# An expert feed-forward stage: first product turned with its weight streamed from DRAM, second product in three rounded passes

## What is computed

```python
xn = (x - mu) * rsqrt(var + EPS) * gamma + beta
probs = softmax(einsum('btd,ed->bte', xn, router_w) / TEMP)
w, idx = top_k(probs, 2)
wdense = sum(one_hot(idx, E) * w[..., None], axis=-2)
h = silu(einsum('btd,edf->betf', xn, W1))
y = einsum('betf,efd->betd', h, W2)
out = einsum('bte,betd->btd', wdense, y) + res
```

## Time and profile before

| | us |
|---|---|
| median of 3 runs | 3400.73 |
| lowest and highest run | 3398.74, 3401.56 |
| span of the profiled execution (first to last instruction) | 3399.2 |
| time of the profiled execution | within the 3 runs above; its profile gives the span alone |
| PE busy in the span | 3002.1 (88%) |
| PE weight loads, DVE, ACT, POOL busy | 1930.5, 1799.6, 1368.2, 1139.2 |
| mean granted clock of TensorE | 0.942 of full |

### The profile page before, as it was taken

One profiled execution on the slowest core, in us unless ns is written; L12 is line 12 of the kernel. 1 busy time (PEld: TensorE's weight loads), 2 busy tenths in 40 slices (PEclk: granted clock), 3 DMA queues, 4 the chain that ended last, 5 costly groups with the idle time before them and its releaser, 6 DMA issues. The chain is left out here.

```text
span 3399.2 us, 47089 instructions
## 1 busy us (share of the span) xinstructions
PE 3002.1 (88%) x17554; PEld 1930.5 (57%) x17554; DVE 1799.6 (53%) x2965; ACT 1368.2 (40%) x2304; POOL 1139.2 (34%) x995
## 2 busy tenths in 40 slices
PE   7779999999999979999988795999687878899877
PEld 6645555555555438888874564766465565344345
DVE  6656565565655654224229654111256758666565
ACT  3334444444444434324323462333232635355554
POOL 0126565665666650000006331333133413121232
PEclk9889999999999989999999896999898899799989
DMA  1100000000000001111100107221200100000000
GB/s 56 53 1 1 1 1 1 1 1 1 1 1 1 1 15 57 50 32 56 50 23 0 35 1 254 34 35 32 53 2 7 28 7 10 2 1 1 1 29 29
DMA packets 108641, 81.89 MB, mean 24 GB/s; under 512 B 22283, under 2 KB 102181, under 8 KB 108421
## 3 DMA queue, kind: packets, MB, share of 16 engines
q1 hardware_dynamic: 94693, 65.15, 6.3%
q0 software_dynamic: 7488, 9.48, 1.7%
q10 hardware_dynamic: 6240, 4.26, 0.4%
HBM read 68.31 MB, written 11.47 MB: 23 GB/s over the span
## 5 line engine op out<-in xcount | busy, mean ns | idle before, releaser
L787 POOL TENSOR_TENSOR acc<-acc,pf 128x512 f32<-128x512 f32 (+1 forms) x448 | 564.0, 1281 | 255.2 <-ACT pf L914 255.2
L971 DVE TENSOR_REDUCE mxa<-ps 128x1 f32<-128x512 f32 x512 | 327.0, 680 | 229.9 <-PE ps L833 227.9
L914 ACT ACTIVATE pf<-ps 128x512 f32<-128x512 f32 x512 | 277.9, 595 | 318.8 <-PE ps L808 293.4
L821 PE MATMUL ps<-pf,v 128*64 128x512 f32 (+1 forms) x1152 | 311.6, 619 | 0.0
L3635 ACT ACTIVATE pT<-ps 128x1024 f32<-128x1024 f32 (+1 forms) x192 | 154.1, 811 | 130.4 <-PE ps L3553 129.8
L3647 DVE TENSOR_REDUCE mx<-ps 128x2 f32<-128x1024 f32 (+1 forms) x192 | 174.8, 950 | 42.4 <-PE ps L3540 36.7
L1168 POOL TENSOR_TENSOR x<-x,ys 128x256 f32<-128x256 f32 x16 | 11.8, 738 | 509.0 <-DVE ys L1373 509.0
L833 PE MATMUL ps<-kH,qH 64*128 64x512 f32 x512 | 158.1, 442 | 23.7 <-DVE mc L979 18.5
L1786 POOL TENSOR_TENSOR e<-e,sm 128x1232 f32<-128x1232 f32 x48 | 107.9, 2247 | 174.6 <-DVE sm L2050 174.6
L2495 DVE TENSOR_SCALAR ys<-ps,xs 128x256 f32<-128x256 f32 x39 | 18.9, 484 | 251.4 <-PE ps L2314 251.4
L811 PE MATMUL ps<-qH,kH 64*128 64x512 f32 (+1 forms) x576 | 144.3, 475 | 1.5 <-ACT pf L914 0.8
(11 more groups left out here) (554 smaller groups left out, 6959.6 us busy)
## 6 DMA issues: line engine op xcount, KB each, us to landing
w_raw<-in_c_h SPq DMA_DIRECT2D x32, 512.0 KB, 4.0
w1a<-in_f_w SPq DMA_DIRECT2D x8, 1024.0 KB, 13.8
w2a<-in_f_w SPq DMA_DIRECT2D x8, 1024.0 KB, 12.8
w_raw<-in_c_w SPq DMA_DIRECT2D x32, 128.0 KB, 2.2
x<-in_x SPq DMA_DIRECT2D x1, 2048.0 KB, 8.4
moe_rows<-rowbuf ACTq DMA_DIRECT2D x4, 512.0 KB, 10.4
moe_acc<-x ACTq DMA_DIRECT2D x1, 2048.0 KB, 13.1
x<-moe_acc SPq DMA_DIRECT2D x1, 2048.0 KB, 8.2
```

What stands on the lines that cost most here:

```text
L787: pool.tensor_tensor(now[0:r, :], now[0:r, :], pf[0:r, n % RING, a, :], ALU.add).then_inc(added.sem, 1)
L821: ins = pe.matmul(g.bk(3)[SIDE[a], :], v[0:r, u // 2 % 2, t, u % 2 * P + a * HD:u % 2 * P + (a + 1) * HD], pf[0:r, n % RING, a, :], start= ...
L914: act.activation(pf[0:r, n % RING, a, :], g.bk(bk.bank[f"s{n}_{a}"])[0:r, :], ACT.Exp, bias=bias)\
L971: dve.tensor_reduce(mxa[:, q % 2, half, a, j:j + 1], g.bk(4 + a), AXX, ALU.max).then_inc(bk.release(f"m{q}_{i}_{a}"), 1)
```

## The change

- `hidden` is turned. W1 is now stationary (128x128 blocks, 16 of them) and the rows `xT` are the moving operand with 128 columns. The product comes out with the hidden dimension on the partitions, so that `turn_hidden` and its PSUM fills are gone. The four PSUM banks 0 to 3 alternate between tiles.
- W1 is no longer held in SBUF. After `indexed`, SP loads the 1 MB W1 of the tile's expert for every tile into a ring of three (`w1r`, events `w1_in`); tile i's load waits for the end of `hidden(i - 3)`. All eight W2 are still loaded at the start.
- `output` takes three passes over rounded parts: with hi the fp32r rounding of a value and lo the fp32r rounding of the rest, it adds h_hi W2_hi, h_hi W2_lo and h_lo W2_hi, 24 matmuls of 256 columns in fp32r.
- ACT makes W2_hi (a copy of the expert's 2048 columns to fp32r) and applies SiLU twice to each half, once to fp32r and once to float32. DVE makes W2_lo and the two halves of h_lo by subtraction.
- PE's order in iteration i is `turn_rows(i + 1)`, `hidden(i)`, `output(i - 1)`. ACT does `rows_out(i + 1)` first, then W2_hi, then the SiLUs. DVE does the three subtractions of tile i before `weighted(i - 1)`.

```diff
@@ -2157,7 +2157,12 @@
-        w1a, w2a = sb("w1a", [P, E8 * KD, H]), sb("w2a", [P, E8 * HB, D])
+        W1_RING = 3
+        w1r, w2a = sb("w1r", [P, W1_RING, KD, H]), sb("w2a", [P, E8 * HB, D])
+        w2s = [sb(f"w2_{n}", [P, 2, HB, D], F32R) for n in ("hi", "lo")]
+        hs = [sb(f"hT_{n}", [P, 2, HB, P], F32R) for n in ("hi", "lo")]
+        PASSES = ((0, 0), (0, 1), (1, 0))
+        f32 = lambda t: t.bitcast(F32)
...
-        h, hT = sb("h", [P, 2, H]), sb("hT", [P, 2, HB, P])
+        h, hT = sb("h", [P, 2 * H]), zT[:].rearrange("p a k n -> p (a k n)").rearrange("p (a f n) -> p a f n", a=2, n=P)
...
         for i in range(N + 1):
-            if i < N:
-                fills += [(f"a{i}_0", 0), (f"a{i}_1", 1)]
             if i + 1 < N:
                 fills += [(f"x{i + 1}", 6 + (i + 1) % 2)]
+            if i < N:
+                fills += [(f"a{i}_0", 2 * (i % 2)), (f"a{i}_1", 2 * (i % 2) + 1)]
             if i:
                 fills += [(f"y{i - 1}", 4 + (i - 1) % 2)]
-            if i < N:
-                fills += [(f"h{i}_0", 2), (f"h{i}_1", 3)]
...
-        first_in, w_in, stored = g.ev("w_loaded", 16 * 3), g.ev("expert_loaded", 32 * E8), g.ev("x_stored", 16)
+        first_in, w_in, stored = g.ev("w_loaded", 16 * 3), g.ev("expert_loaded", 16 * E8), g.ev("x_stored", 16)
...
+        w1_in = [g.ev(f"raw_loaded{r}", 16 * len(range(r, N, W1_RING))) for r in range(W1_RING)]
+        w2_hi, w2_lo, h_lo = g.ev("w_hi_made", N), g.ev("w_lo_made", N), g.ev("g_lo_made", 2 * N)
...
@@ -2221,8 +2226,13 @@
                 for e in range(E8):
-                    load(sp, w1a[:, e * KD:(e + 1) * KD, :], rows(W1[e]), w_in)
                     load(sp, w2a[:, e * HB:(e + 1) * HB, :], rows(W2[e]), w_in)
+                sp.wait_ge(*indexed.at(0, 1))
+                for i in range(N):
+                    e = sp.value_load(texp[0:1, i:i + 1], min_val=0, max_val=E8 - 1)
+                    if i >= W1_RING:
+                        sp.wait_ge(*bk.full(f"a{i - W1_RING}_1", 0))
+                    sp.dma_start(w1r[:, i % W1_RING], W1[ds(e, 1)].rearrange("a (k p) n -> p (a k) n", p=P)).then_inc(w1_in[i % W1_RING].sem, 16)
...
@@ -2287,32 +2297,28 @@
-                def hidden(i, e):
+                def hidden(i):
                     pe.wait_ge(*bk.read(f"x{i}", 0))
+                    pe.wait_ge(*w1_in[i % W1_RING].at(0, 16 * (i // W1_RING + 1)))
                     for half in range(2):
+                        out = g.bk(2 * (i % 2) + half)
                         pe.wait_ge(*bk.free(f"a{i}_{half}", 0))
-                        for k in range(KD):
-                            ins = pe.matmul(g.bk(half), xT[:, i % 2, k, :],
-                                            w1a[:, ds(e * KD + k, 1), half * CH:(half + 1) * CH].rearrange("p a n -> p (a n)"),
-                                            start=k == 0, stop=k == KD - 1)
-                        ins.then_inc(bk.fill(f"a{i}_{half}"), 1)
-
-                def turn_hidden(i):
-                    for half in range(2):
-                        pe.wait_ge(*bk.read(f"a{i}_{half}", 0))
-                        pe.wait_ge(*bk.free(f"h{i}_{half}", 0))
                         for f in range(HB // 2):
                             at = half * CH + f * P
-                            ins = pe.transpose(g.bk(2 + half)[:, f * P:(f + 1) * P], h[:, i % 2, at:at + P], g.ident[:])
-                        ins.then_inc(bk.fill(f"h{i}_{half}"), 1)
-
-                def output(i, e):
+                            for k in range(KD):
+                                ins = pe.matmul(out[:, f * P:(f + 1) * P], w1r[:, i % W1_RING, k, at:at + P], xT[:, i % 2, k, :],
+                                                start=k == 0, stop=k == KD - 1)
+                        ins.then_inc(bk.fill(f"a{i}_{half}"), 1)
+
+                def output(i):
                     pe.wait_ge(*bk.free(f"y{i}", 0))
+                    pe.wait_ge(*w2_lo.at(0, i + 1))
                     for f in range(HB):
                         if f % (HB // 2) == 0:
-                            pe.wait_ge(*bk.read(f"h{i}_{f // (HB // 2)}", 0))
-                        ins = pe.matmul(g.bk(4 + i % 2)[:, 0:D], hT[:, i % 2, f, :],
-                                        w2a[:, ds(e * HB + f, 1), :].rearrange("p a n -> p (a n)"), start=f == 0, stop=f == HB - 1)
+                            pe.wait_ge(*h_lo.at(0, 2 * i + f // (HB // 2) + 1))
+                        for p, (sh, sw) in enumerate(PASSES):
+                            ins = pe.matmul(g.bk(4 + i % 2)[:, 0:D], hs[sh][:, i % 2, f, :], w2s[sw][:, i % 2, f, :],
+                                            start=f == 0 and p == 0, stop=f == HB - 1 and p == len(PASSES) - 1)
@@ -2340,19 +2346,13 @@
-                pe.wait_ge(*w_in.at(0, 32 * E8))
-                last = None
                 for i in range(N + 1):
-                    if i < N:
-                        e = pe.value_load(texp[0:1, i:i + 1], min_val=0, max_val=E8 - 1)
-                        hidden(i, e)
                     if i + 1 < N:
                         turn_rows(i + 1)
+                    if i < N:
+                        hidden(i)
                     if i:
-                        output(i - 1, last)
-                    if i < N:
-                        turn_hidden(i)
-                        last = e
@@ -2387,18 +2387,22 @@
+                act.wait_ge(*w_in.at(0, 16 * E8))
+                act.wait_ge(*indexed.at(0, 1))
                 for i in range(N):
+                    if i + 1 < N:
+                        rows_out(i + 1)
+                    e = act.value_load(texp[0:1, i:i + 1], min_val=0, max_val=E8 - 1)
+                    if i >= 2:
+                        act.wait_ge(*bk.full(f"y{i - 2}", 0))
+                    act.activation(w2s[0][:, i % 2], w2a[:, ds(e * HB, HB), :], ACT.Copy).then_inc(w2_hi.sem, 1)
                     for half in range(2):
+                        at, src = slice(half * (HB // 2), (half + 1) * (HB // 2)), g.bk(2 * (i % 2) + half).rearrange("p (f s) -> p f s", s=P)
                         act.wait_ge(*bk.full(f"a{i}_{half}", 0))
                         if i >= 2:
-                            act.wait_ge(*bk.full(f"h{i - 2}_{half}", 0))
-                        act.activation(h[:, i % 2, half * CH:(half + 1) * CH], g.bk(half), ACT.Silu).then_inc(bk.release(f"a{i}_{half}"), 1)
-                    if i + 1 < N:
-                        rows_out(i + 1)
-                    act.wait_ge(*bk.full(f"h{i}_0", 0))
-                    if i >= 2:
-                        act.wait_ge(*bk.full(f"y{i - 2}", 0))
-                    act.activation(hT[:, i % 2, 0:HB // 2, :], g.bk(2).rearrange("p (f s) -> p f s", s=P), ACT.Copy).then_inc(bk.release(f"h{i}_0"), 1)
+                            act.wait_ge(*h_lo.at(0, 2 * (i - 2) + half + 1))
+                        act.activation(hs[0][:, i % 2, at, :], src, ACT.Silu)
+                        act.activation(hT[:, i % 2, at, :], src, ACT.Silu).then_inc(bk.release(f"a{i}_{half}"), 1)
@@ -2495,21 +2499,30 @@
+                def weights_low(i):
+                    e = dve.value_load(texp[0:1, i:i + 1], min_val=0, max_val=E8 - 1)
+                    dve.wait_ge(*w2_hi.at(0, i + 1))
+                    dve.tensor_tensor(w2s[1][:, i % 2], w2a[:, ds(e * HB, HB), :], f32(w2s[0][:, i % 2]), ALU.subtract).then_inc(w2_lo.sem, 1)
+                    return e
+
+                def hidden_low(i, half):
+                    at = slice(half * (HB // 2), (half + 1) * (HB // 2))
+                    dve.wait_ge(*bk.read(f"a{i}_{half}", 0))
+                    dve.tensor_tensor(hs[1][:, i % 2, at, :], hT[:, i % 2, at, :], f32(hs[0][:, i % 2, at, :]), ALU.subtract).then_inc(h_lo.sem, 1)
+
                 last = None
                 for i in range(N + 1):
+                    if i < N:
+                        now = weights_low(i)
+                        hidden_low(i, 0)
+                        hidden_low(i, 1)
                     if i:
                         weighted(i - 1, last)
-                    if i < N:
-                        last = dve.value_load(texp[0:1, i:i + 1], min_val=0, max_val=E8 - 1)
-                        dve.wait_ge(*bk.full(f"h{i}_1", 0))
-                        if i >= 2:
-                            dve.wait_ge(*bk.full(f"y{i - 2}", 0))
-                        dve.tensor_scalar(hT[:, i % 2, HB // 2:, :], g.bk(3).rearrange("p (f s) -> p f s", s=P), 1.0, None, ALU.mult)\
-                            .then_inc(bk.release(f"h{i}_1"), 1)
+                    last = now
```

More of the change, by code:

```diff
@@ L2182, in stage_l1_ffn @@
         xs, xT = sb("xs", [P, RING, MOE_ROW]), sb("xT", [P, 2, KD, P])
-        h, hT = sb("h", [P, 2, H]), sb("hT", [P, 2, HB, P])
+        h, hT = sb("h", [P, 2 * H]), zT[:].rearrange("p a k n -> p (a k n)").rearrange("p (a f n) -> p a f n", a=2, n=P)
         ys = sb("ys", [P, 2, D])
```

(18 more changed lines are left out.)

## The result

The changed kernel takes 3432.0 us (median of four runs, 3420.75 to 3436.15) against 3400.95 us of the kernel before, a ratio of 1.0086 with a 95% interval of 1.0068 to 1.0104. It is slower by 31 us; 3364 us, faster, was predicted. The profiled execution took 3436.15 us, with a span of 3434.4 us.

What follows compares the result with a forecast made beforehand. TensorE's own instructions were taken to bound the tile loop. From the 3399.2 us span, -38.2 (tiles) - 0.5 (ends) + 2 (gathers) = -37 gave 3362.5; with 1.5 us from span to median, 3364 us, range 3358 to 3389 us.

Steps and rivals of the forecast that it cites:

- The turn of the hidden rows, -0.87 us a tile: On TensorE, the turn of the hidden rows goes, saving 0.87 us a tile.
- Second product, 2.88 us: On TensorE, 24 fp32r matmuls at 0.120 us take 2.88 us instead of 3.46, so -0.58 us a tile.
- First product, 3.90 us: On TensorE, 32 records at 0.122 us take 3.90 us, +0.47 us a tile; 3.43 us kept as lower end.
- A tile of TensorE's own work, 7.00 us: In the tile loop, TensorE needs 7.00 us a tile against 7.98, saving 38.2 us over 39 tiles.
- ScalarE 5.3 us, VectorE 4.2 us, hidden: Per tile, ScalarE's 5.3 us and VectorE's 4.2 us of work stay hidden behind TensorE's 7.00 us.
- The weight's landing at the start and in the loop: First 1 MB W1 load lands near 2106.5 us, costing 1 us (0 to 3); three buffers cover later loads.
- It costs nothing by itself: Streaming 1 MB of W1 per tile has no bandwidth problem: 2.7 of 7.0 us.
- Now it is within half a microsecond of TensorE's own 7.0: Output-to-gather-to-turn loop: 6.4 us at the median landing, 7.5 at the maximum; before, 1.6 us to spare.
- 2 us for gathers that slip: In the tile loop, late gathers add 2 us in all; most tiles take 7.0 us.
- The period cannot be below 3.6 + L: Tile period is at least 3.6 us plus the gather's landing time, since rows are needed one tile later.
- GpSimd and VectorE shut each other out: Rival: VectorE's 2.29 us subtraction holds the gather, period 8.7 us, 3428 us; 6% with other slowing waits.
- First rival, L = 3.9, 3382 us: Gather landing of 3.9 us every tile makes the period 7.5 us, gain 19 us; 31% including partial blocking.

Runs made afterwards that it cites:

- gather_first: Changed kernel with GpSimd's gather moved ahead of the scatter, four gathers ahead of the loop in place of three; 3350.1 us.
- no_both: Changed kernel with W1 loaded for the first three tiles only and W2's low part made for the first two tiles only; 3347.7 us.
- no_w2lo: Changed kernel with VectorE's subtraction for W2's low part made for the first two tiles only, W1 still streamed; 3378.7 us.
- no_stream: Changed kernel with W1 loaded for the first three tiles only, all engine instructions kept; 3381.6 us.
- fp32_second: Changed kernel with the second product left in fp32 on the resident W2, without high and low parts; 3405.2 us.

## Why the prediction was wrong, step by step

- **The turn of the hidden rows, -0.87 us a tile:** right; it is gone and nothing came in its place.
- **Second product, 2.88 us:** right. The timeline steps by 0.120 us, and the loops with and without the passes differ by 0.61 us a tile.
- **First product, 3.90 us:** mis-sized, on the careful side. The loads of one, and the first load behind them, in the changed kernel (timeline of PEld):
```profile
2247.14 3.65 PEld L2309 LDWEIGHTS ps<-xT,w1r 128*128 128x128 f32 x32
2250.71 0.19 PEld L2320 LDWEIGHTS ps<-w_hi,hT_hi 128*128 128x128 f32 x1
```
  32 loads in 2250.71 - 2247.14 = 3.57 us are 0.112 us each. The value lies between the two ends that I kept, 3.43 and 3.90 (0.122 us a load); a step measured at 136 columns had been taken for one at 128.
- **A tile of TensorE's own work, 7.00 us:** 6.66 measured (in gather_first turns start at 2246.50, 2253.16 and 2259.82). The gain in work is 39 x (7.98 - 6.66) = 51.5 us instead of 38.
- **ScalarE 5.3 us, VectorE 4.2 us, hidden:** right. In the changed kernel ScalarE has 1.91 + 4 x 0.60 + 0.81 = 5.1, VectorE 2.29 + 2 x 0.69 + 0.48 = 4.2, and TensorE waits for neither.
- **The weight's landing at the start and in the loop:** right to within 1 us. The first `hidden` starts at 2106.66 (before: 2106.53), and no wait for `w1r` stands among the waits of the loop.
- **The stream, "It costs nothing by itself":** wrong. That TensorE never waits for `w1r` bears out the bandwidth, but the stream lies in the gather's way: alone it costs 31 us over no_both.
- **"Now it is within half a microsecond of TensorE's own 7.0", 2 us for gathers that slip:** the step that failed. The place was named correctly, with 3.5 us from output to gather (at 2209.23 and 2212.72: 3.5), and so was the reason, the turn moved ahead of the first product. The size of L, the landing of the gather, was not: I took the 2.8 us of a quiet queue although I had written that streams and gathers would overlap, and 6.0 to 6.7 us came in about every second tile. So the 2 us for late gathers stood against 54 us of waits. The maximum of 3.9 us was misread too: it is the gather at 2380.33 us, long after the weights had landed. The one issued while weights still moved, the first, took 3.8 us. Not 38 but 32 of the 39 gathers needed 3.3 us or less; the last six needed 3.5 to 3.9 in the quiet. No row of before had a gather that met the start of a 1 MB load, or one that was held.
- **"The period cannot be below 3.6 + L":** wrong in form. A gather starts 3.5 us behind an output and its rows must be there one whole tile later. If TensorE waits G within that tile, the tile is longer by G and the rows have G more time, so the next wait is G(next) = 3.5 + L - 6.66 - G, not below 0. With a wait in one tile there is then none in the next, and the waits come in every second tile only. The rule fits the sizes: L = 4.0 gives 0.84 (measured 0.68 and 0.72 in no_w2lo), 6.0 gives 2.84 (2.75), 8.4 gives 5.24 (5.12).
- **The clock:** it was absent from the sum, since the loop had no waits before. Waits of up to 1.7 us left the clock at 1.00 (no_stream, 2110 to 2350 us). Longer ones mostly cost, but not in step with their length: in the changed kernel the first product lost 1.1 us after 2.75 us and 2.4 us after 3.39 us, but nothing after the waits of 2.62 and 2.85 us that ended at 2127.44 and 2345.46; in fp32_second it lost 2.7 us after 2.60 us. The extra busy time of the changed loop over gather_first is 294.0 - 262.6 = 31 us; with the 54.5 us of waits that is 86 us, and less the gain in work of 51.5 us it leaves 34, the loss of the loop (33 us) but for its ends.
- **The rival "GpSimd and VectorE shut each other out":** its mechanism was there, with the gather 0.3 us inside the subtraction, and its 3428 us lies 4 us beside the result, but that is partly luck. It wanted L = 5.1 in every tile. What happened is L = 6.0 to 6.7, once 8.4, in about every second tile. That "a longer tile moves the gather to an earlier place in the next one, before the subtraction" was true, and hence the alternation; but one held gather in two is enough, once the stream and the clock add to it. The subtraction's hold alone, without the stream, stays a gain (3381.6 us). A chance of 6% for it was much too low: the gather had been placed "just at its edge", that of the subtraction, and half a microsecond of slack was all that stood against it.
- **First rival, L = 3.9, 3382 us:** the kernel without the low part came near it in time (3378.7 us), with landings of mostly 3.6 to 4.7 us in about every second tile. That it wanted L = 3.9 in every tile was wrong, as with the other rival.

## What to carry to other kernels

When a change shortens the tile and moves a consumer forward, write down for each gathered buffer the time between its trigger and its deadline, and price its latency beside the new traffic, not in the quiet kernel; here a gather that met a 1 MB load landed some 0.8 us after the load's end. Two small delays on the same gather, here a hold and a stream, nearly add up as waits (23 and 25 us alone, 52 together), but cost more than their sum in time, since waits of around 3 us mostly cost TensorE again in its clock and those of 1.7 us and less did not. A change that comes out slower may be a good one with one instruction in the wrong place: moving the gather ahead of the scatter made this one 3350 us, 1.6% faster than the kernel before.

## What had not been expected of the hardware

An indirect transfer's instruction on GpSimd, 0.99 us alone, ends about 0.86 us after a VectorE instruction that reads two tensors from SBUF (2.29 us), and also waits for a fast one that reads one tensor (2047 columns in 1.22 us), but not for a reduction of 2048 columns to one (2.29 us). A row gather whose instruction ended 0.9 us or less before a 1 MB load began to move lands only some 0.8 us after the load's end, and one gather of the 39 later still. fp32 matmuls of 128 columns, each with a fresh 128x128 weight, follow each other in 0.112 us a record.
